# Eight pieces of expert weights, each taken one shared-expert block earlier

## What is computed

```python
x = x + tanh(g_xattn) * attention(layernorm(x), keys and values from ctx and x)
h = layernorm(x)
p = softmax(h @ gate_w.T)                    # 8 experts, the best 2 of each token
routed = sum over its 2 experts of p_e * ((silu(h @ fc1_e.T) * (h @ fc2_e.T)) @ proj_e.T)
shared = (silu(h @ sfc1.T) * (h @ sfc2.T)) @ sproj.T       # hidden width 704
x = x + tanh(g_ffn) * (routed + sigmoid(h @ shared_gate.T) * shared)
```

## Time and profile before

| | us |
|---|---|
| median of 3 runs | 286.82 (286.31 to 286.86) |
| the profiled execution, device time | 286.08 |
| its span, first to last instruction | 284.3 |
| busy: PE, DVE, ACT, POOL | 271.9, 209.7, 164.2, 134.6 |
| mean granted TensorE clock, as a share of full speed | 0.996 |

### The profile page before, as it was taken

How to read it: one execution, slowest core, us unless ns; L and a number is a source line. 1 busy time by engine, 2 the same in 40 slices (tenths; PEclk the granted TensorE clock), 3 DMA queues, 4 the chain that set the end, 5 groups by cost and what they waited for, 6 DMA issues and landing times.

```text
span 284.3 us, 5839 instructions
## 1 busy us (share of the span) xinstructions
PE 271.9 (96%) x1788; PEld 246.7 (87%) x1788; DVE 209.7 (74%) x683; ACT 164.2 (58%) x369; POOL 134.6 (47%) x160
## 2 busy tenths in 40 slices
PE   3999999999999999999999999999999999999994
PEld 3799889889897777898788888899999999998883
DVE  6959767888778779578767858777777878763365
ACT  2875687777455395652245555567676666654330
POOL 2241913714575555663430000087787878776140
PEclk9999999999999999999999999999999999999998
DMA  7452263130046226424335653578887888766796
GB/s 198 186 190 86 75 221 94 59 131 0 23 110 250 78 76 211 154 68 127 127 91 203 221 182 101 161 122 135 139 135 139 134 138 135 119 71 71 265 399 227
DMA packets 25022, 40.18 MB, mean 141 GB/s; under 512 B 2976, under 2 KB 18976, under 8 KB 24992
## 3 DMA queue, kind: packets, MB, share of 16 engines
q1 hardware_dynamic: 16272, 27.43, 30.1%
q0 software_dynamic: 7152, 9.57, 19.9%
q10 hardware_dynamic: 1568, 2.80, 2.7%
HBM read 22.68 MB, written 17.11 MB: 140 GB/s over the span
## 4 chain that ended last, share of the span: by engine, by line
PE 81%; DVE 7%; DMA 5%; ACT 4%; issue 2%; ACTq 0%; DVEq 0%
PE bank L441 62%; PE bank L718 7%; DMA ew_hi<-y_d 3%; PE bank L449 3%; PE bank L817 3%; PE bank L771 3%; DVE work L1482 2%; ACT sh_hi L848 1%; DVE sh_lo L1119 1%; DMA consts_sb<-consts_dram 1%; PE bank L528 1%; ACT ew_hi L848 1%; DVE ew_lo L1119 1%; PE bank L598 1%; ACT work L1028 1%
## 5 line engine op out<-in xcount | busy, mean ns | idle before, releaser
L1685 POOL DMA_INDIRECT y_d<-work,dest_of_slot x39 | 60.5, 1552 | 55.4 <-DMA y_d<-work 38.9
L441 PE MATMUL bank<-ew_hi,xt_hi 128*128 (+2 forms) x172 | 53.9, 323 | 1.1 <-DVE xt_lo L1119 0.7
L441 PE MATMUL bank<-ew_lo,xt_hi 128*128 (+2 forms) x172 | 51.7, 301 | 0.0
L441 PE MATMUL bank<-ew_hi,xt_lo 128*128 (+1 forms) x133 | 40.6, 305 | 0.0
L1645 POOL DMA_INDIRECT xs_d<-xn_all,slot_of_pair x32 | 33.8, 1057 | 10.2 <-issue 7.3
L1119 DVE TENSOR_TENSOR xt_lo<-bank,xt_hi 128x256 fp32r<-128x256 f32 (+2 forms) x90 | 35.6, 397 | 3.6 <-ACT xt_hi L848 2.4
L441 PE MATMUL bank<-xt_hi,sw_hi 128*128 128x512 f32 x88 | 34.8, 395 | 0.2 <-issue 0.2
L848 ACT ACTIVATE xt_hi<-bank 128x256 fp32r<-128x256 f32 (+1 forms) x90 | 32.9, 410 | 2.9 <-PE bank L817 1.1
L441 PE MATMUL bank<-xt_lo,sw_hi 128*128 128x512 f32 x88 | 34.5, 392 | 0.0
L441 PE MATMUL bank<-xt_hi,sw_lo 128*128 128x512 f32 x88 | 34.3, 390 | 0.0
L441 PEld LDWEIGHTS bank<-ew_hi,xt_hi 128*128 128x128 f32 (+1 forms) x172 | 32.4, 189 | 1.8 <-DVE xt_lo L1119 0.9
(11 more groups left out here) (163 smaller groups left out, 667.3 us busy)
## 6 DMA issues: line engine op xcount, KB each, us to landing
work<-xs_d SPq DMA_DIRECT2D x39, 136.0 KB
weight_stage<-ew_dram SPq DMA_DIRECT2D x10, 486.5 KB, 3.6
y_d<-work SPq DMA_DIRECT2D x6, 512.0 KB
work<-ctx_t_dram SPq DMA_DIRECT2D x4, 512.0 KB, 3.2
ew_hi<-y_d ACTq DMA_DIRECT2D x4, 512.0 KB, 7.1
ew_hi<-y_d SPq DMA_DIRECT2D x4, 512.0 KB, 7.9
xn_all<-x_dram SPq DMA_DIRECT2D x3, 512.0 KB, 6.0
xs_d<-pad_row SPq DMA_DIRECT2D x9, 136.0 KB, 2.4
```

The lines of the kernel that those rows point to most:

```text
L441: last = nc.tensor.matmul(dst, a, b, start=(n == 0), stop=(n == len(pairs) - 1))
L1685: nc.gpsimd.indirect_dma_start(out=y2_d, out_offset=bass.IndirectOffsetOnAxis(ap=IX[:, n:n + 1], axis=0), in_=EY[:, n % 4, :], in_offset=None,
```

## The change

One tuple of constants changes. `PIECE_AT[n]` is the block behind which ACT and DVE split piece n. Pieces 0 and 1 stay; pieces 2 to 9 each take the entry before their old one, with (1, 2) new at the front and (2, 4) gone at the end. Two pieces still share (2, 1): 6 and 7 now, 5 and 6 until now. Block (1, 2) also has the last part of the table on DVE.

```diff
-PIECE_AT = ((0, 2), (0, 4), (1, 3), (1, 4), (1, 5), (2, 1), (2, 1), (2, 2), (2, 3), (2, 4))
+PIECE_AT = ((0, 2), (0, 4), (1, 2), (1, 3), (1, 4), (1, 5), (2, 1), (2, 1), (2, 2), (2, 3))
```

## The result

The changed kernel took 291.79 us (median of 6 runs, 290.67 to 293.16) against 286.91 (6 runs, 286.31 to 287.68): 4.9 us more, a ratio of 1.0175 with a 95% interval of 1.0152 to 1.0198. Slower was forecast, and the time lies inside the range of 289.0 to 293.6. The 292.8 that was given as the likeliest is 1.0 too high.

What follows compares the result with a forecast made beforehand. TensorE, busy for 96% of the span, was taken as the bound, so only its waits count. Switch -0.69, wait +4.80 and clock +1.85 made +5.96 us, from 286.82 to 292.8, range 289.0 to 293.6.

Steps and rivals of the forecast that it cites:

- The gain at the switch: Shared to routed experts: without the tenth piece at (2, 4), TensorE's whole wait for DVE goes, -0.69 us.
- The front: Piece 2 at (1, 2): low half ends at 144.91; no cost at once, small lateness swallowed by the later wait.
- SP and the wait: Load 5, behind the pads on SP, lands at 157.45; TensorE's projection of (2, 0) comes 4.80 us later.
- The second rival: Shorter wait at (2, 0): load 5 lands in 3.4 us, wait 3.50, or 2.9 with evenly spaced pads; chance 0.10.
- The clock: TensorE's clock falls in the wait ahead of (2, 0): +1.85 us, the middle of 1.43 and 2.28.
- The rival in which the clock holds: The wait ahead of (2, 0) is there but the clock stays at its high level: 290.9 us; chance 0.28.
- The sum: Whole kernel: -0.69 + 4.80 + 1.85 = +5.96 us, 292.8 us on the median of 286.82.

Runs made afterwards that it cites:

- the pads behind load 5: The changed kernel with the eight pad stores behind load 5 instead of load 4 on SP: 286.19 us against 286.58, ratio 0.9990.
- the filled variant: The changed kernel with 33 identity transposes on TensorE inside its wait ahead of the projection of (2, 0): 289.75 us against 286.58, ratio 1.0126.
- Both ways of freeing load 5 by a step too many: Against the changed kernel: sixth piece at (2, 0) instead of (1, 5), 288.65 us, again 288.57; or pads behind load 6, 289.03 us.
- the front undone: The changed kernel with pieces 2 and 3 back at (1, 3) and (1, 4), piece 4 second at (1, 4): 294.82 us against 286.58, ratio 1.0288.

## Why the prediction was right

**The gain at the switch: -0.69 forecast, -0.69 in the trace.** With the tenth piece gone from (2, 4), the first routed product follows the projection without a wait, in the changed kernel and in every variant with its list.

**The front: nothing at once, small lateness swallowed.** Right in the changed kernel. Piece 2's low half ended at 145.45, which is 144.81 less the 0.64 of this execution, against the 144.91 forecast. The lateness cost 0.61 us in the profile of the pads behind load 5, where nothing swallows it.

**SP and the wait: +4.80 forecast, +4.08 in the trace.** Every link is there: load 4 earlier, pads at once behind it, load 5 behind the pads, ACT, DVE, the sums, PE. Undoing the order on SP alone takes the loss away, and holding the loads back by 1.9 us more makes it larger. The size was off mainly in one term: load 5 landed in 3.8 us and not 4.7 (-0.9); the 1.60 us of SP's own instruction did not recur. The way from load 4 to load 5 was 8.04 us and not 7.76 (+0.28), and load 4 itself was 0.1 us earlier than forecast: -0.72 in all. The forecast took the one execution's 4.7 as the load's price. The second rival was nearer with its 3.4, and had too little weight. The fit of the Trainium skill's page "DMA: Bandwidth & Descriptors", section "Anatomy of one DMA", given there for GpSimd's path, made 3.1 us as an estimate; the 3.8 measured here, on a load that SP issues, lies between it and the forecast.

**The clock: +1.85 forecast, +2.32 in the trace.** The case that was taken, a fall, is the one that came, and the loss is just above the upper bound of 2.28 that the start of the trace had given; the forecast's middle of the two bounds was too low. Filling the wait took 2.34 us away between the marks and 1.7 at the medians. The rival in which the clock holds, 290.9, fell with it: no run of the changed kernel was under that but one, at 290.67. The Trainium skill's page "TensorE: Matmul & The Clock Gate", section "Why this matters for your kernels", says that an idle gap between bursts of matmuls puts the array back to half rate; this trace agrees, with 0.50 granted behind an idle time of 3.89 us.

**The sum: +5.96 forecast, +5.71 between the marks in the profiled execution, +4.9 at the medians.** The two misses, -0.72 and +0.47, nearly cancel in the trace, and that is luck. Why the medians lie lower is not shown. The clock may have a part in it: over the six runs the mean granted clock is 0.987 to 0.994, and the two longest have the lowest (0.987 at 293.16, 0.988 at 292.81). But the third longest, 292.19, has 0.994, and the mean also takes in a fall behind PE's last matmul, as in the earlier trace rows, when PE has no work left. The forecast, like the profiled execution, is near the dear end. How much of the 4.9 is the clock at the median is known only from the filled variant: 1.7, and 3.2 for the wait less what the switch won.

## What to carry to other kernels

When a piece of work is moved earlier, follow the load that feeds it back through its issuing queue and look for what stands between that load and the one before: here the piece moved up by two blocks' time, while its load moved up by only 2.1 us (155.01 against 153.57 less 0.64), since eight stores kept their place ahead of it. A wait that two engines hand on shows up under the last one's name, so read the bracket on each engine of the chain until a DMA or the queue is named. And price a stall of TensorE of several us with the time that its clock takes to come back, half as much again here.

## What the runs showed that was not expected

A late load does not end with one wait. Both ways of freeing load 5 by a step too many made load 7 the late one (ACT waited 1.67 and 2.87 us), and only one place of the pads among three left no load late enough to hold PE up: behind load 5.

SP's own pace is uneven. One and the same load took 1.60 us of SP in the kernel before and 0.38 in the changed one, and there the eight pads follow each other at 0.82 to 1.24 us, of which the store's instruction is some 0.33. The register read in front of each (line 388) takes another 0.26 to 0.58, as the chain that ended last has it, since it now leads through SP:

```profile
149.77 0.27 SPq L388
150.07 0.04 SPq L389
...
150.22 0.33 SPq L390
```

The clock's loss came from an idle time of 3.9 us, and the low level outlasted it: it was granted for 1.7 us of the wait and 5.1 us of work. With the front undone the same fall came later, 3.6 us after PE stopped (159.6 to 163.2) and not 2.2, where the earlier trace rows have it 1.3 us after the last matmul; so it can't be foretold from one trace when the fall comes.
